# Reciprocals of softmax denominators folded over all partitions by DMAs, in a four-stage attention chain

## The reference, cut to what matters

```python
scores = jnp.einsum('bhqd,bhkd->bhqk', q * scale, k)
attn = jax.nn.softmax(scores, axis=-1)
o = jnp.einsum('bhqk,bhkd->bhqd', attn, v)
```

## Time and profile before

| | us |
|---|---|
| median of 3 runs (lowest, highest) | 516.5 (515.22, 517.43) |
| the profiled execution | 514.55 |
| its span, first to last instruction | 512.8 |
| busy: PE, DVE, ACT, POOL | 479.3, 360.1, 273.3, 217.8 |
| idle of POOL before L425, released by DVE L692, in layer 0 | 61.4 |
| DVE L692 on den_sb, 128x64 x48 | 25.6 |
| layer 0, 1, 2 start their maxima at | 22.7, 187.4, 347.8 |

### The profile page before, as it was taken

How to read it: one execution, slowest core, us unless ns; L and a number is a source line. 1 busy time by engine, 2 the same in 40 slices (tenths; PEclk the granted TensorE clock), 3 DMA queues, 4 the chain that set the end, 5 groups by cost and what they waited for, 6 DMA issues and landing times.

```text
span 512.8 us, 7031 instructions
## 1 busy us (share of the span) xinstructions
PE 479.3 (93%) x2268; PEld 238.7 (47%) x2268; DVE 360.1 (70%) x687; ACT 273.3 (53%) x522; POOL 217.8 (42%) x203
## 2 busy tenths in 40 slices
PE   8799999999989899999999999999999989998996
PEld 6454444443237565444444322664544444432463
DVE  7599888976164568987887823738988787832573
ACT  3138776767514324876766762131777765764032
POOL 8300021001000002898879991000699888896000
PEclk9969999999998998999999999998999999999999
DMA  5330432000000054487944440034457854442002
GB/s 145 56 57 20 137 65 34 1 2 2 1 0 1 15 123 104 82 203 159 207 89 84 83 79 5 1 88 109 92 120 154 182 105 83 84 83 42 1 0 82
DMA packets 16419, 38.18 MB, mean 74 GB/s; under 512 B 4870, under 2 KB 6030, under 8 KB 16256
## 3 DMA queue, kind: packets, MB, share of 16 engines
q1 hardware_dynamic: 11088, 21.72, 17.7%
q0 software_dynamic: 5152, 16.00, 16.9%
q10 hardware_dynamic: 144, 0.02, 0.0%
HBM read 4.76 MB, written 1.05 MB: 11 GB/s over the span
## 4 chain that ended last, share of the span: by engine, by line
PE 68%; DVE 15%; DMA 4%; ACT 4%; issue 3%; SPq 3%; POOL 2%; ACTq 0%; POOLq 0%; DVEq 0%
PE PV L927 15%; PE S L889 15%; PE S L916 11%; DVE max L662 10%; PE S L1037 4%; DMA k_stack<-kL 4%; PE M L943 3%; PE PV L844 2%; PE S L870 2%; DVE rec_sb L692 2%; PE M L870 2%; PE PV L870 2%; PE S L907 2%; PE S L1082 2%; PE PV L863 1%
## 5 line engine op out<-in xcount | busy, mean ns | idle before, releaser
L662 DVE TENSOR_REDUCE max<-S 128x1 f32<-128x512 f32 x384 | 239.8, 669 | 20.8 <-PE S L889 20.6
L514 ACT ACTIVATE E<-S 128x512 f32<-128x512 f32 x384 | 212.6, 601 | 76.2 <-PE S L916 72.2
L450 POOL TENSOR_TENSOR SUMS<-E 128x512 f32<-128x512 f32 x126 | 167.0, 1476 | 123.9 <-ACT E L514 123.8
L889 PE MATMUL S<-k_stack,q_stack 126*128 126x512 f32 x384 | 183.2, 490 | 13.5 <-DVE max L662 8.7
L916 PE MATMUL S<-q_stack,k_stack 128*128 128x512 f32 x384 | 154.6, 411 | 2.7 <-ACT E L514 1.5
L889 PEld LDWEIGHTS S<-k_stack,q_stack 126*128 126x128 f32 x384 | 74.4, 194 | 92.9 <-DVE max L662 64.7
L927 PE MATMUL PV<-E,V 128*32 128x512 f32 x768 | 95.4, 599 | 1.7 <-ACT pv_sb L521 1.7
L916 PEld LDWEIGHTS S<-q_stack,k_stack 128*128 128x128 f32 x384 | 72.6, 191 | 33.3 <-ACT E L514 20.6
L692 DVE RECIPROCAL rec_sb<-den_sb 128x64 f32<-128x64 f32 (+1 forms) x54 | 35.7, 665 | 35.0 <-ACT den_sb L531 35.0
L503 ACT ACTIVATE mHL<-S 4x128 fp32r<-4x128 f32 x48 | 12.6, 263 | 55.2 <-PE S L907 55.2
L927 PEld LDWEIGHTS PV<-E,V 128*32 128x32 f32 x768 | 20.0, 109 | 45.2 <-issue 28.3
(11 more groups left out here) (180 smaller groups left out, 335.5 us busy)
## 6 DMA issues: line engine op xcount, KB each, us to landing
SUMS<-SUMS POOLq DMA_DIRECT2D x30, 512.0 KB, 5.1
k_stack<-kH SPq DMA_DIRECT2D x32, 128.0 KB, 3.0
q_stack<-qH SPq DMA_DIRECT2D x40, 64.0 KB, 2.0
k_stack<-kL SPq DMA_DIRECT2D x16, 128.0 KB, 3.2
q_stack<-qH SPq DMA_DIRECT2D x16, 128.0 KB, 2.3
q_stack<-mHL SPq DMA_DIRECT2D x96, 2.0 KB
q_stack<-qL SPq DMA_DIRECT2D x20, 64.0 KB, 2.0
X<-x_in_dram SPq DMA_DIRECT2D x2, 512.0 KB, 5.5
```

What stands on the lines that cost most here:

```text
L450: pool.tensor_tensor(SUMS[:, slot, :], E[:, E_PLAN[s][0], :], E[:, E_PLAN[s + 1][0], :], ALU.add).then_inc(sum_ready, 1)
L514: act.activation(E[:, slot, :], B[:, ring_of_scores(s) % B_RING, :], ACT.Exp, scale=1.0 if l == 0 else float(HEAD_DIM[l]) ** -0.5).then_in ...
L662: dve.tensor_reduce(max8[:, m % 2, r:r + 1], A[:, n % A_RING, :], AX.X, ALU.max, negate=True).then_inc(a_used, 1)
L889: pe.matmul(A[:, n % A_RING, :], q_stack[0:SHIFT_ROW, slot, q0:q0 + P], k_stack[0:SHIFT_ROW, slot, k0:k0 + HALF], start=True, stop=True).t ...
```

## The change

For blocks 0 and 1 of each layer the four denominator rows (4x512) are laid out as 128 partitions x 16 columns by a DMA (`fold_sums`), DVE takes one reciprocal of 128x16 at step 64 (and one at step 96), a second DMA writes the 16-column result back as four rows of den_sb, and a third reads these four rows and writes them to all 128 partitions of rec_sb (`spread_reciprocals`). In layer 0 the fold reads pv_sb itself, so the products L957 of blocks 0 and 1 and ACT's copies of their results go. In layers 1 and 2 ACT's copy of M moves from steps 59, 91 and 123 to 54, 86 and 118. Blocks 2 and 3 keep their reciprocals. SP waits inside its stream: for pv_sb or den_sb before the fold, for DVE's reciprocal, and for the second DMA before the third.

```diff
@@ -320,6 +328,28 @@
+            def fold_sums(l, b):
+
+                if l == 0:
+                    sp.wait_ge(pv_out, pv_count(l, b))
+                    src, row = pv_sb, DP // 2
+                else:
+                    sp.wait_ge(den_out, den_count(l, b))
+                    src, row = den_sb, 0
+                sp.dma_start(den_in[:, :], src[row:P:DP, :].rearrange("u (d n) -> u d n", n=PER_ROW)).then_inc(dens_folded, 16)
+
+            def spread_reciprocals(l, b):
+
+                n = FOLDED * l + b + 1
+                sp.wait_ge(recs_folded, n)
+                sp.dma_start(den_sb[0:P:DP, :].rearrange("u (d n) -> u d n", n=PER_ROW), rec_out[:, :]).then_inc(recs_rows, 16)
+                sp.wait_ge(recs_rows, 16 * n)
+                sp.wait_ge(att_ready, (BLOCKS - 1) * l + b)
+                sp.wait_ge(att_tail, 2 * l)
+                sp.dma_start(rec_sb[:, :],
+                             den_sb[0:P:DP, :].rearrange("u (o n) -> u o n", o=1)
+                             .to_broadcast([HEADS_B, DP, HALF])).then_inc(recs_spread, 16)
@@ -360,11 +390,16 @@
                     load_k(sp, l, h)
                     if h < SLOTS:
                         shift_rows(l, h + 1)
+                fold_sums(l, 0)
                 if l == 1:
                     sp.wait_ge(proj_done, UNIT0[2])
                     sp.dma_start(W12[:, :, 0:3 * C], w2[:, :, 0:3 * C]).then_inc(w_in[2], 16)
                 for j in range(9, UNITS_L):
                     shift_rows(l, j)
+                    if j in (9, 13):
+                        spread_reciprocals(l, (j - 9) // HEADS_B)
+                    if j == 12:
+                        fold_sums(l, 1)
@@ -421,7 +456,10 @@
-                pool.wait_ge(rec_ready, rec_count(l, b))
+                if b < FOLDED:
+                    pool.wait_ge(recs_spread, 16 * (FOLDED * l + b + 1))
+                else:
+                    pool.wait_ge(rec_ready, rec_count(l, b))
@@ -523,11 +561,11 @@
-                if l + b:
-                    act.wait_ge(rec_ready, rec_count(l, b - 1) if b else REC_L * l)
+                act.wait_ge(recs_spread, 16 * (FOLDED * l + min(b, FOLDED)))
+                act.wait_ge(rec_ready, REC_L * l)
                 act.activation(den_sb[:, :], M[:, :], ACT.Copy).then_inc(den_out, 1)
@@ -564,9 +602,10 @@
-                    den_step = 59 if l else 62
-                    if s >= den_step and (s - den_step) % 32 == 0:
-                        denominators_out(l, (s - den_step) // 32)
+                    den_step = 54 if l else 62
+                    b = (s - den_step) // 32
+                    if s >= den_step and (s - den_step) % 32 == 0 and (l or b >= FOLDED):
+                        denominators_out(l, b)
@@ -675,20 +714,24 @@
+            def folded_reciprocals(l, b):
+
+                n = FOLDED * l + b
+                dve.wait_ge(dens_folded, 16 * (n + 1))
+                dve.wait_ge(recs_rows, 16 * n)
+                dve.reciprocal(rec_out[:, :], den_in[:, :]).then_inc(recs_folded, 1)
@@ -738,11 +781,10 @@
-                    b, part = (s - REC_STEP) // 32, (s - REC_STEP) % 32 // 2
-                    if 0 <= b < 2 and s % 2 == 0 and part < REC_PARTS[b]:
-                        reciprocals(l, b, part)
-                for part in range(REC_PARTS[2]):
-                    reciprocals(l, 2, part)
+                    if s >= REC_STEP and (s - REC_STEP) % 32 == 0 and (s - REC_STEP) // 32 < FOLDED:
+                        folded_reciprocals(l, (s - REC_STEP) // 32)
+                for part in range(2):
+                    reciprocals(l, BLOCKS - 2, part)
                 last_block(l)
@@ -1008,8 +1050,8 @@
-                    if l == 0 and s >= 60 and (s - 60) % 32 == 0:
-                        gather_sums((s - 60) // 32)
+                    if l == 0 and s == 60 + 32 * FOLDED:
+                        gather_sums(FOLDED)
```

More of the change, by code:

```diff
@@ L44 @@
 W_COLS = (3 * 128 + C, 4 * C, 4 * C)
-REC_PARTS = (8, 8, 2, 2)
+FOLDED = 2
 REC_STEP = 64
+PER_ROW = HALF // DP
 LEAD_GROWTH = (1, 3, 5, 7)
@@ L130, in attention_chain @@
         spare = sb("spare", [P, 2])
+        den_in = sb("den_in", [P, PER_ROW])
+        rec_out = sb("rec_out", [P, PER_ROW])
         mv = sb("mv", [P, KC, 2])
@@ L195, in attention_chain @@
         rec_ready, att_ready, att_tail = sem("rec_ready"), sem("att_ready"), sem("att_tail")
+        dens_folded, recs_folded, recs_rows, recs_spread = (sem("dens_folded"), sem("recs_folded"), sem("recs_rows"),
+                                                            sem("recs_spread"))
         out_done, x_ready = sem("out_done"), sem("x_ready")
@@ L252, in sum_count @@
             return (l - 1) * SUMS_L + min(PAIRS * j + k + 1, SUMS_L)
-        REC_L = sum(REC_PARTS)
         RING_L = STEPS + UNITS_L
@@ L265, in attention_chain, with den_count @@
         IN_RING.update({ring_of_scores(s): ("scores", s) for s in range(STEPS)})
+        REC_L = 2 * (BLOCKS - FOLDED)
+        PV_OUTS = (4, 3, 3)
+        DEN_OUTS = (BLOCKS - 1 - FOLDED, BLOCKS - 1, BLOCKS - 1)
         def rec_count(l, b):
-            return REC_L * l + sum(REC_PARTS[:b + 1])
-        PV_OUTS, DEN_OUTS = (4, 3, 3), 3
+            return REC_L * l + 2 * (b - FOLDED + 1)
+        def den_count(l, b):
+            return sum(DEN_OUTS[:l]) + b + 1 - (0 if l else FOLDED)
         def pv_count(l, b):
@@ L525, in denominators_out @@
                 if l == 0:
-                    act.wait_ge(gathered, b + 1)
+                    act.wait_ge(gathered, b - FOLDED + 1)
                 else:
                     act.wait_ge(den_done, DENS_L * (l - 1) + 2 * (b + 1))
-                if l + b:
-                    act.wait_ge(rec_ready, rec_count(l, b - 1) if b else REC_L * l)
+                act.wait_ge(recs_spread, 16 * (FOLDED * l + min(b, FOLDED)))
+                act.wait_ge(rec_ready, REC_L * l)
                 act.activation(den_sb[:, :], M[:, :], ACT.Copy).then_inc(den_out, 1)
@@ L676, in low_rows @@
                                   mHL[:, m % 2, 0, :].bitcast(F32), ALU.subtract).then_inc(rows_low, 1)
+            def folded_reciprocals(l, b):
[3 more added lines that the diff above has]
+                dve.reciprocal(rec_out[:, :], den_in[:, :]).then_inc(recs_folded, 1)
             def reciprocals(l, b, part):
-                wide = HALF // REC_PARTS[b]
-                cs = slice(wide * part, wide * (part + 1))
+                cs = slice(QUARTER * part, QUARTER * (part + 1))
                 if part == 0:
@@ L684, in reciprocals @@
                     if b < BLOCKS - 1:
-                        dve.wait_ge(den_out, DEN_OUTS * l + b + 1)
+                        dve.wait_ge(den_out, den_count(l, b))
                     elif l == 0:
-                        dve.wait_ge(gathered, BLOCKS)
+                        dve.wait_ge(gathered, BLOCKS - FOLDED)
                     else:
                         dve.wait_ge(den_done, DENS_L * l)
-                    if b == 0 and l:
-                        dve.wait_ge(att_tail, 2 * l)
                 dve.reciprocal(rec_sb[:, cs], den_sb[:, cs] if b < BLOCKS - 1 else M[:, cs]).then_inc(rec_ready, 1)
@@ L699, in last_block @@
                     dve.wait_ge(pv_done, PAIRS_L * (l + 1))
-                    dve.wait_ge(rec_ready, REC_L * l + sum(REC_PARTS[:-1]) + part + 1)
+                    dve.wait_ge(rec_ready, rec_count(l, BLOCKS - 2) + part + 1)
                     dve.tensor_tensor(att[:, KC - 1, HALF + QUARTER * part:HALF + QUARTER * (part + 1)], PV[:, cs],
@@ L934, in denominators @@
                 if k == 0 and b:
-                    pe.wait_ge(den_out, DEN_OUTS * l + b)
+                    pe.wait_ge(den_out, den_count(l, b - 1))
                 first = HEADS_B * b
@@ L954, in gather_sums @@
                 pe.wait_ge(pv_out, b + 1)
-                if b:
-                    pe.wait_ge(den_out, b)
+                if b > FOLDED:
+                    pe.wait_ge(den_out, b - FOLDED)
                 pe.matmul(M[:, :], gather[:, :], pv_sb[:, :], start=True, stop=True).then_inc(gathered, 1)
```

## The result

The changed kernel takes 525.9 us (four runs, 522.8 to 529.9), the kernel before on the same chips 516.3. The ratio is 1.019, its 95% interval 1.0116 to 1.0265: slower by about 10 us, where 3.6 less was forecast, and above the range of 509.6 to 518.5. The profiled execution took 526.88, its span is 525.1.

A forecast was written before the change was run, and what follows sets the result against it. The chain of waits was 68% PE and 15% DVE, so DVE time counts only on the chain. Layer 0 -3.9, layer 1 +0.4, layer 2 -0.1 gave -3.6: 516.5 to 512.9 us, range 509.6 to 518.5.

The forecast's parts named there:

- Layer 0: Steps 53 to 109: removed products and DVE pieces gain 1.97 + 1.90 = 3.9 us, fold hidden.
- The gains of layers 1 and 2: Removed DVE pieces gain 0.78 in steps 69 to 77 and 0.71 in 93 to 109; 1.3 counted per layer.
- The fold's wait: DVE at step 64, layers 1 and 2: fold lands at 255.6 behind a load, costing 1.2 each (ends 0 and 5.0).
- the price of the way back in layers 1 and 2: Write-back, spread, then maxima rows before step 80: stall 0.5 in layer 1 (ends 0 and 2), none in layer 2.
- The rate: 0.131 a piece: Spread's 32 pieces on each of four engines at SP's queue price of 0.131 us take 4.2.
- The contention: Spread in layers 1 and 2 shares engines with GpSimd's accumulating DMAs: 5.4 instead of layer 0's 4.2.
- the weights of layer 1: Next layer's weights, queued before the write-back, land about 259.7, so the write-back is seen then instead of at 258.4.
- Step 112: PE's need of second-block maxima rows: 16 steps leave 12.5; no stall in the forecast sum.
- rival 3: Slower: spread pieces cost 0.269, maxima rows late at steps 80 and 112; +7.9, 524.4; chance 0.15 with milder forms.
- ACT's copy: Step 118, copy of M (0.67 us) now ahead of PV's copy: counted zero (ends 0 and 0.67 a layer).
- The rule of the Trainium skill on the number of engines: Spread from four source rows is confined to four engines; otherwise it would end 3 us sooner, changing no term.

The follow-up runs named there:

- the one with thin sums: Changed kernel with the accumulating DMAs of units 8, 9, 10, 12 and 13 in layers 1 and 2 moving an eighth of the bytes: 515.6 us, ratio 1.0003.
- the spread cut by heads: Changed kernel with the spread issued as four DMAs, one per head, each from one row to its 32 partitions: 537.9 us, ratio 1.0425.
- the fastest kernel: Changed kernel with sixteen source rows, spread behind next maxima rows, copies at 59, 91, 123, later reciprocals in layers 1 and 2, later weights: 509.7 us, ratio 0.989.

## Why the prediction was wrong

**Layer 0** was right in each of its gains: the two products, the pieces of block 0 (the interval of 7.25 became 6.45) and of block 1; 3.8 measured for 3.9. The fold was hidden, the reciprocal took 0.23, and the spread was there by 93.6, when GpSimd began, 9.1 after DVE's step 64 where 9.2 was worked out. That last agreement is luck: the write-back was seen at 2.1 instead of 2.8 (its 0.4 for short pieces has no row, and 32 of the prediction's own 20 ns would be 0.6), and the spread took 7.1 instead of 6.4.

**The gains of layers 1 and 2** were right too: the interval 70 to 78 fell from 7.24 to 6.46, and 94 to 110 from 13.17 to 12.49, 0.68 for 0.71. The fold's wait, taken at 1.2, lengthened its interval by 0.33 and 0.35 in the profiled run. I had put the fold 0.4 behind the landing of the load ahead of it. In layer 1 the two landed together (the fold at 254.36; the load, issued at 248.98, 5.4 later), in layer 2 the fold came first (421.36 against 416.24 + 5.7). So the landing of the load is no floor for the fold, and DVE idled 1.34 and 0.91 instead of 2.4.

**The step that failed** is the price of the way back in layers 1 and 2. I put the write-back at t + 2.8 in layer 2 and it was seen at t + 4.77; I put the spread and the rows behind it at 7.6 + 0.3 from issue to release, and they took 9.57 in layer 2 and 10.96 in layer 1. In layer 2 the rows were so 3.6 late against the sum, 2.0 from the write-back and 1.7 from the spread. Three things were in it. The rate: 0.131 a piece came from the mean of a queue, most of whose DMAs read from 16 or more partitions at once; an engine that reads one row again and again took about 0.17 (5.6 us for 32), which is 1.4 more than the 4.2 I took, and in layer 0 the allowance for issue and landing covered it. The contention: I added 1.2 to the spread for it, and with GpSimd's DMAs cut down spread and rows took 7.75 instead of 9.57 in layer 2, so it was 1.8 there. The write-back I had priced as if alone. It took 4.47 from its issue in layer 2, and 4.08 even with the cut, which leaves whole the DMA of unit 7 that ran beside it; at step 96 of both layers it took 1.84, with a share of 0.10 and 0.08 of the DMA engines busy meanwhile, against 0.65 here. And the weights of layer 1. The 259.7 forecast for the write-back against 259.6 measured is luck: the weights landed at 257.2 (issued at 251.99, 5.2), not at 259.7, and leaving them out of the way made the write-back only 0.9 shorter. The rows came at t + 16.2 and t + 14.3, step 80 was due at t + 11.9 and t + 11.8, near the 11.7 of the forecast.

**Step 112** I had called hidden, with rows at t + 10.7 against 12.5; there they came late by 1.65 and 1.90. Half of this is the spread again: it and the rows took 10.1 and 10.4 instead of 7.9, though the write-back took only 1.84, and the rows came at t + 12.2 and t + 12.5. The other half is the 12.5: PE stood ready at t + 10.6 in both layers. The 12.5 is the distance of PE's own steps 96 and 112, but t is DVE's reciprocal, which comes later than PE's step 96; in the sum for step 80 the same 16 steps were rightly 11.7 and not 12.9. With 12.5 these rows would have been just in time. (In rival 3 the 2.3 for layer 1 at t + 12.6 should be 2.1, by the rival's own terms; nothing hangs on it.)

**A term was missing**: the clock behind a stall. Each stall of PE was counted as long as it lasts. The 4.31 at step 80 cost 6.0, and the 1.90 of layer 2 was followed by sixteen products L985 that took 3.21 instead of 1.85 and eight of L969 that took 1.94 instead of 1.06, in a stretch that lost 3.7. The added cost is not certain: a wait of 2.54 cost 2.7 in layer 2 of the changed kernel, at 1.00 behind it, and 4.3 in layer 1 of the one with thin sums, at 0.59.

**ACT's copy**, counted zero, cost 0.3 in four places. I looked for its price at step 118, where nothing happened, and not at the interval 54 to 62. Why the copy costs more ahead of PV's copy than behind it the runs don't show.

The third rival named the place where PE stops, and its chance of 0.15 was too low. It had been turned down because "SP's own packets cost half of that", a mean over DMAs of another shape. That its 524.4 is near the 525.9 is in good part luck: it took 0.269 a piece where 0.17 was measured, had layer 0 lose 2.2 and 1.4 where nothing was lost, and had neither the slow write-back nor the clock. The rule of the Trainium skill on the number of engines (page "DMA: Bandwidth & Descriptors", section "Why a DMA increments its semaphore by 16 and not by 1") agrees with the share of 0.24 of the engines in layer 0. What I read into it, that more engines would by themselves shorten the spread by 3 us, was refuted by the spread cut by heads; with sixteen source rows as well it came true.

**Open.** Layer 0's end, from step 110 to layer 1, took 66.4 before, 67.7 in the changed kernel, and from 66.2 to 69.1 in the others with an identical layer 0. In the changed kernel the stretch of the layer norm has a granted clock of 0.63 where it was 1.00 before:

```profile
153.00:160.00 7.00, 6.41 (x38) 6.32 (x38) 0.93 (x3) 1.49 (x3) 0.00 (x0) 0.63 0.00 0
```

It varies among executions of kernels that are alike there, so I don't put it down to the change; whether a shorter layer 0 makes it more likely wasn't tried. Layer 1's start (its first maxima rows to step 46), 46.0 before and 47.7 in the changed kernel's profiled run, was 46.0 to 46.8 in all the others but one, and 47.7 in the fastest kernel, so it isn't put down to the change either. These two and 0.3 in layer 0 are 3.3 of the 12.3 us between the two profiled spans.

## What to carry to other kernels

A DMA that replaces work of a busy engine must be priced with what stands behind it in its queue: here 256 KB were never late for their reader, but 2 KB behind them were, by up to 4.3 us. Issuing the large one behind the small one won back more than the whole loss. So did a spread from sixteen source rows instead of four, at the price of three more small writes. Count the time that is left for a reader from the event that starts the DMA, not from another engine's step number. And where PE may stand still, add the slower clock that can follow to the price.

## What the runs showed of the hardware

- Source rows of SBUF read again and again: from four rows, with a share of 0.24 of the 16 engines, 49 GB/s; from one row at a time, with a share of 0.77, 35; from sixteen rows up to 212. The transfer was always 128 pieces of 2 KB into 128 partitions, and landed 3.1 us after its issue in the last case. Whether the number of the rows or their place counts wasn't tried.
- A small DMA (8 KB in 128 pieces) issued by SP came back after 1.84 us in layer 0 (84.74 to 86.58) and at step 96 of layers 1 and 2, where 0.10 of the DMA engines or less were busy; after 4.1 to 4.5 beside one of GpSimd's 512 KB accumulating DMAs (shares of 0.65 to 0.71), and after 5.0 and 6.0 where a load of 768 KB of weights stood before it as well.
- A pause of PE of 1.45 us was followed by 22 products in 4.57 us at a granted clock of 0.63 (both levels of 1.2 and 2.4 GHz within the stretch), and one of 1.49 by the same products in 3.08 us at 1.00. A pause of 1.53 was followed by either. The length of a pause alone doesn't tell which it will be.
- DVE's reciprocal took 0.23 us for 128x16 against 0.53 for 128x64 and 1.75 for 128x256.
